# Order of VectorE's additions and of the last sums in a two-layer attention and FFN kernel

## The chip, the cores and the metric

The kernel runs on one core of one Trainium2 chip. The metric is the device time of one execution in microseconds. The core has five engines with a queue each: TensorE (PE; PEld is its weight load), VectorE (DVE), ScalarE (ACT), GpSimd (POOL) and SyncE (SP), which here issues all DMAs. Each works its queue strictly in order, and semaphores alone order one queue against another.

## The reference

2048 tokens (32 batches of 64) of width 512 pass through four stages, each with a layer norm and a residual:

```python
x = x + L0_xattn(layernorm(x), ctx, ctx, mask)          # 32 q heads, 8 kv heads, rope, softmax
x = x + L0_ffn(layernorm(x), 4-bit weights)             # silu(gate) * up, width 1376
x = x + L1_xattn(layernorm(x), ctx, mask)               # rms-normed q and k
x = x + L1_ffn(layernorm(x), ...)                       # h + gate[..., None] * aux_out
```

The last stage looks up the 8 best of 128 slots for each token (`aux_out`) and scales them with a gate that depends on a mean over all tokens. `hidden_states` there is the normed X.

## The kernel before

**Tiling.** X stays in SBUF as 16 tiles of 128 tokens x 512, named (c, t): chunk c of 512 tokens (0 to 3), tile t (0 to 3). Products of two 32-bit values are made of f16 parts, a high one and a residue ("low"), in three products. ScalarE writes the high parts, VectorE or GpSimd the residues. PB are the 8 banks of PSUM.

**The first attention** is 32 units, each a kv head g and a chunk c, software-pipelined: beside unit u the front of unit u + 1 is done. TensorE's order in one step is: `scores(u)` (L937), keys and values of u + 1 (L868, L880), the four `queries` of u + 1 (L912), the four tiles of `output(u - 1, t)` (L960), `weigh(u)` (L1002). An output tile t goes to bank 2, 3, 0, 2, and `bank()` makes TensorE wait until the last reader of a bank is through: for a tile of output this is VectorE's addition to X (`output` of VectorE, L2355). `weigh` uses banks 0, 1, 6 and 7.

Each query h is rotated: ScalarE turns it (L1547, L1548), VectorE multiplies by the cosine (L2191), GpSimd by the sine (L2962) and adds (`queries_0` of GpSimd, L2967), ScalarE makes the high part (L1554), VectorE the residue (`queries_0` of VectorE, L2200, both inputs in SBUF). `scores` of u + 1 waits for the residues 0 and 1 in its first half, 2 and 3 in its second. The softmax takes a maximum and an exponent (ScalarE, L1608) and a reciprocal.

**Work beside units** is put in by hand into numbered slots, `plan(L, u, slot, stage, ...)`; `side(L, u, slot)` in each engine's program does its part. Slot 0 is behind keys, 1 to 4 behind each query, 5 to 8 behind each output tile, 9 at the end of the unit. So `plan_ln(L, u, i, c)` puts layer norm i of chunk c into unit u, in two halves of two tiles: `ln_norm` (ScalarE, L1649, writes LNB, after GpSimd's LNR and LNK, L2946 and L2948), `ln_turn` (TensorE transposes LNB, L1031; ScalarE writes the high part of XT, L1661) and `ln_low` (VectorE, the residue of XT out of the same bank, L2158). For layer norm 1 of chunk 0, in unit 30, the second half uses banks 1 and 6. Unit 2 and unit 4 hold layer norm 0 of chunks 2 and 3. Low halves of contexts and weights are L2136.

**The end** (`last_tail`). Chunk 3 goes through the last stage tile by tile (`r_...`), the others by chunk (`t_...`). `t_norm_tile` of GpSimd (L3084) adds the normed value to X. When the gates are made (`GR`, L2638), each of the 16 tiles becomes X + GR x result. VectorE does 12, in one operation each (`t_out`, L2650): for chunks 0 and 1 the result lies in SBUF (CTB), for 2 and 3 in PSUM. Four are done by TensorE (`BY_PE`): the identity times X (L1233) and a diagonal of GR times the result (L1235) into one bank; ScalarE makes the diagonal (L1830) and copies the bank to X (L1834). The picks of chunk 3 (`r_pick`, L2666 to L2674) lie between. SP then issues one output DMA of 256 KB for each tile, in the fixed order `OUT_ORDER`, waiting for each (L832).

Of the kernel before, what the change touches and what calls it, by code (L numbers as in the profile page):

```python
# [13 lines left out]
ALU = mybir.AluOpType  # L14
# [73 lines left out]
def build(nc, din, out):  # L88
    ctx = ExitStack()
    with ctx:  # L90
# [228 lines left out]
        def eco(L, g, n):  # L319
# [34 lines left out]
        k_pow, k_mul, sql, q_pow, x_add2, tail_one = \  # L354
            [signal(n) for n in ("k_pow", "k_mul", "sql", "q_pow", "x_add2", "tail_one")]
# [76 lines left out]
        def plan_ln(L, u, i, c, early=True, last=6):  # L432

            if early:
                plan(L, u - 1, 9, "ln_stats", i, c)
            for half, (norm, turn, low) in enumerate(((0, 2, 2), (3, 5, last))):
                plan(L, u, norm, "ln_norm", i, c, half)
                plan(L, u, turn, "ln_turn", i, c, half)
                plan(L, u, low, "ln_low", i, c, half)
# [38 lines left out]
        plan_ln(0, 30, 1, 0, last=7)  # L478
# [41 lines left out]
        BY_PE = [(0, 0), (0, 2), (1, 0), (1, 2)]  # L520
        BY_DVE = [(c, t) for c in range(3) for t in range(4) if (c, t) not in BY_PE]
        SUM_BANK = {x: (7, 4)[i % 2] for i, x in enumerate(BY_PE)}
        DIAG = {x: words(128 * i, 128) for i, x in enumerate(BY_PE)}
        OUT_ORDER = [(0, 1), (0, 3), (0, 0), (1, 1), (1, 3), (0, 2), (2, 0), (1, 0), (2, 1), (2, 2), (1, 2), (2, 3)]
        OUT_ORDER += [(3, t) for t in range(4)]

# [151 lines left out]
        def sync(sp):  # L678
# [151 lines left out]
            for c, t in OUT_ORDER:  # L830
                sp.wait_ge(*((x_out, (c, t)) if (c, t) in BY_PE else (fin, (c, t))))
                sp.do.dma_start(ov[:, 4 * c + t, :], X[:, 4 * c + t, :]).then_inc(out_done.of("out", 16), 16)  # L832
# [4 lines left out]
        def tensor(pe):  # L837
# [522 lines left out]
            def last_tail():  # L1360
# [35 lines left out]
                t_out(2, 2)  # L1396
                t_sum(*BY_PE[1])
                t_out(2, 3)
                t_out(3, 2)
                t_out(3, 3)  # L1400
                t_sum(*BY_PE[2])
                t_sum(*BY_PE[3])
# [56 lines left out]
        def scalar(act):  # L1459
# [408 lines left out]
            def front(L, u, beside):  # L1868

                if L == 0:  # L1870
                    if u > 1:
                        turned_k(u)
                    exponent(0, beside)
# [200 lines left out]
        def vector(dve):  # L2074
# [615 lines left out]
            def front(L, u, beside):  # L2690
                if (L, u) != (1, 1):
                    unit_scale(L, u)
                if L == 0:
                    if u > 1:
                        turned_k(u)
                    soft_sum(0, beside)
                    if u > 1:
                        values_0(u)
                    keys_0(u)
                    side(0, beside, 0)  # L2700
                    for h in range(4):
                        turned_q(u, h)
                        if (beside, h) == (0, 3):
                            turned_p(0, 0)
                        if h == 2:
                            halved_p(0, beside, 1)
                        if h in (2, 3):
                            queries_0(u, h - 2)
                        side(0, beside, 1 + h)
                else:  # L2710
                    if beside > 0:
                        values_1(u, 0)
                        soft_sum(1, beside)
                        values_1(u, 1)
                    else:
                        soft_sum(1, 0)
                    side(1, beside, 0)
                    for h in range(4):
                        queries_1(u, h)
                        side(1, beside, 1 + h)  # L2720

            def units(L):
                for u in range(NU - 1):
# [13 lines left out]
                    for t in range(4):  # L2737
                        if u > 0:
                            output(L, u - 1, t)
                        if L == 0 and t == 0:  # L2740
                            queries_0(u + 1, 2)
# [57 lines left out]
            def last_tail():  # L2799
# [29 lines left out]
                for c, t in BY_DVE:  # L2829
                    if c < 2:  # L2830
                        t_out(c, t)
                t_out(2, 0)
                t_out(2, 1)
# [87 lines left out]
        def gpsimd(pool):  # L2921
# [167 lines left out]

            STAGE = {"join_x": join_x, "fold_x": fold_x, "fold_w": fold_w, "fold_w_halves": fold_w_halves,  # L3090
# [73 lines left out]
            def last_tail():  # L3164
# [7 lines left out]
                t_norm_tile(3, 3)  # L3172

# [99 lines left out]
```

## Time and profile before

| what | value |
|---|---|
| runs, us | 2393.34, 2393.75, 2394.59 (median 2393.75) |
| profiled execution, us | 2390.72 |
| its span, first to last instruction, us | 2388.9 |
| mean granted TensorE clock, share of full | 0.997 |
| busy PE, DVE, ACT, POOL | 98%, 73%, 54%, 54% |
| TensorE busy, 60 to 1000 us | 926.21 of 940 us |
| TensorE busy, 2345 to 2389 us | 34.17 of 44 us |
| bytes moved by DMA | 116.60 MB |

A group of instructions in the profile is a line, engine and operation; "out<-in" gives tiles. The time in brackets ahead of an instruction is its engine's idle time and what ended it; "issue" is idle time for which the trace finds no releaser. The end of a row is its start plus its duration.

### The profile page before, as it was taken

The page shows a single profiled execution, that of the slowest core. Times are in us where ns is not written, and L with a number is a line of the kernel's source. Part 1 is how long each engine was busy: PE and PEld are TensorE (multiplying, and loading weights), DVE is VectorE, ACT ScalarE, POOL GpSimd, SP SyncE. Part 2 cuts the span into 40 slices and gives each one's busy share as a digit, 9 for nine tenths or more (in the row PEclk, how much of TensorE's full clock was granted, in tenths as well). Part 3 has the DMA queues.
Part 4 walks back from the last instruction along what each step waited for, and adds up shares of the span by engine and source line. Part 5 has one row for each costly group of instructions (what it writes and reads, how often), then busy time and mean ns, then how long its engine had stood idle before and what let it go on. Part 6 is the DMA issues. An engine that isn't in the chain of part 4 may idle for free.

```text
span 2388.9 us, 46219 instructions
## 1 busy us (share of the span) xinstructions
PE 2348.3 (98%) x18028; PEld 1327.5 (56%) x18028; DVE 1740.7 (73%) x3256; ACT 1288.9 (54%) x2511; POOL 1299.4 (54%) x1042
## 2 busy tenths in 40 slices
PE   8899999999999999999999999999999999999998
PEld 4555555555555555444666655555555555555554
DVE  8887887878887898756887666666666666766666
ACT  7666565656555555424454564555555555544454
POOL 4656566666666666237763454445555555445631
PEclk9999999999999999999999999999999999999999
DMA  6121121312121111110102011222121212221101
GB/s 214 45 45 36 45 54 28 124 27 54 28 58 32 43 40 27 29 44 28 36 29 101 27 32 28 45 54 63 36 63 37 63 37 63 54 43 28 28 14 71
DMA packets 217912, 116.60 MB, mean 49 GB/s; under 512 B 169408, under 2 KB 192608, under 8 KB 216672
## 3 DMA queue, kind: packets, MB, share of 16 engines
q1 hardware_dynamic: 217696, 113.64, 18.9%
q8 instruction: 145, 2.38, 0.4%
q14 instruction: 71, 0.58, 0.1%
HBM read 65.81 MB, written 8.39 MB: 31 GB/s over the span
## 4 chain that ended last, share of the span: by engine, by line
PE 79%; DVE 9%; POOL 4%; ACT 4%; issue 3%; DMA 0%; SPq 0%; DVEq 0%; POOLq 0%; ACTq 0%
PE PB L960 24%; PE PB L912 22%; PE PB L896 6%; PE PB L1072 5%; PE PB L1129 4%; PE PB L937 3%; PE PB L1002 3%; PE PB L1083 2%; PE PB L868 2%; PE PB L880 2%; POOL AR L2962 1%; DVE AR L2340 1%; PE PB L981 1%; DVE WB L2136 1%; POOL AR L2967 1%
## 5 line engine op out<-in xcount | busy, mean ns | idle before, releaser
L960 PE MATMUL PB<-WB,AR 128*128 128x512 f16 x3072 | 682.5, 379 | 2.0 <-DVE X L2355 1.6
L912 PE MATMUL PB<-XTB,WB 128*128 128x512 f16 x3072 | 679.1, 380 | 2.6 <-DVE WB L2136 1.5
L960 PEld LDWEIGHTS PB<-WB,AR 128*128 128x128 f16 x3072 | 296.9, 98 | 356.0 <-DVE X L2355 5.0
L912 PEld LDWEIGHTS PB<-XTB,WB 128*128 128x128 f16 x3072 | 297.6, 98 | 346.6 <-issue 6.5
L2973 POOL TENSOR_TENSOR AR<-AR,SML 128x512 f32<-128x512 f32 x128 | 144.8, 1152 | 315.3 <-DVE SML L2325 315.3
L2355 DVE SCALAR_TENSOR_TENSOR X<-PB,SML,X 128x512 f32<-128x512 f32 x256 | 188.8, 746 | 165.3 <-PE PB L960 159.3
L1638 ACT ACTIVATE AR<-PB 128x512 f16<-128x512 f32 x256 | 131.6, 597 | 230.7 <-PE PB L1002 230.4
L2229 DVE TENSOR_TENSOR AR<-PB,AR 128x512 f16<-128x512 f32 x128 | 88.2, 690 | 165.1 <-ACT AR L1601 165.1
L2962 POOL TENSOR_TENSOR AR<-AR,CST 128x512 f32<-128x512 f32 x128 | 190.9, 1491 | 31.5 <-ACT AR L1548 31.5
L2967 POOL TENSOR_TENSOR AR<-AR 128x512 f32<-128x512 f32 x128 | 177.2, 1385 | 11.7 <-DVE AR L2191 1.9
L2953 POOL TENSOR_TENSOR AR<-AR,CST 128x512 f32<-128x512 f32 x32 | 49.1, 1535 | 236.2 <-ACT AR L1527 236.1
L1554 ACT ACTIVATE AR<-AR 128x512 f16<-128x512 f32 x128 | 80.5, 630 | 176.3 <-POOL AR L2967 174.8
L896 PE MATMUL PB<-WB,CTB 128*128 128x256 f16 x1536 | 173.1, 273 | 0.1
L2340 DVE TENSOR_TENSOR AR<-PB,AR 128x512 f16<-128x512 f32 x256 | 158.6, 681 | 12.8 <-ACT AR L1638 12.7
L2191 DVE TENSOR_TENSOR AR<-PB,CST 128x512 f32<-128x512 f32 x128 | 88.1, 689 | 107.7 <-ACT AR L1548 107.7
L3011 POOL TENSOR_TENSOR SML<-SML 128x16 f32<-128x16 f32 (+1 forms) x33 | 98.2, 2975 | 121.3 <-DVE SML L2237 121.3
L2200 DVE TENSOR_TENSOR AR<-AR 128x512 f16<-128x512 f32 x128 | 144.8, 1132 | 22.2 <-ACT AR L1554 22.2
L896 PEld LDWEIGHTS PB<-WB,CTB 128*128 128x128 f16 x1536 | 147.9, 98 | 17.6 <-DVE X L2355 0.4
L3003 POOL TENSOR_TENSOR AR<-AR 128x512 bf16<-128x512 f32 x128 | 147.1, 1159 | 16.1 <-ACT AR L1601 16.0
L2982 POOL TENSOR_TENSOR PSP<-AR,PSP 128x512 f16<-128x512 f32 x93 | 118.9, 1292 | 0.0
L1508 ACT ACTIVATE WB<-STG,SML 128x512 f16<-128x512 f32 (+1 forms) x164 | 92.8, 644 | 22.2 <-PE PB L960 17.4
L937 PE MATMUL PB<-AR 128*128 128x64 f16 x3072 | 102.5, 194 | 2.0 <-DVE AR L2200 2.0
(313 smaller groups left out, 4114.7 us busy)
## 6 DMA issues: line engine op xcount, KB each, us to landing
STG<-in_wo SPq DMA_DIRECT2D x14, 1024.0 KB
STG<-in_wq SPq DMA_DIRECT2D x13, 1024.0 KB
STG<-in_qw_gu SPq DMA_DIRECT2D x40, 128.0 KB
STG<-in_ctxT SPq DMA_DIRECT2D x4, 1024.0 KB
X<-in_x SPq DMA_DIRECT2D x4, 1024.0 KB, 10.5
kept<-CTB SPq DMA_DIRECT2D x4, 1024.0 KB, 7.3
CTB<-kept SPq DMA_DIRECT2D x4, 1024.0 KB, 6.5
out_x<-X SPq DMA_DIRECT2D x16, 256.0 KB, 2.4
```

Of the source, the lines that this page charges most:

```text
L896: m = pe.do.matmul(b[:, t2 * 256:(t2 + 1) * 256], CT[x][c][:, k, tok], wkv[y][:, k, :], start=n == 0, stop=n == 11)
L912: m = pe.do.matmul(b[:, :], wq[x][:, k, h * 128:(h + 1) * 128], XT[y][c][:, k, :], start=n == 0, stop=n == 11)
L937: m = pe.do.matmul(bk[:, b * SQ:(b + 1) * SQ], rows_of(QT[x], pair, b), KTT[y][:, b * SQ:(b + 1) * SQ], start=n == 0 and not by_pe, stop=n ...
L960: m = pe.do.matmul(b[:, :], AT[x][:, h, t * 128:(t + 1) * 128], wo[y][:, h, :], start=n == 0, stop=n == 11)
L1638: act.do.activation(hi, b[:, :].rearrange("p (b h q) -> p b h q", b=2, h=4), copy).then_inc(at_hi.of((L, u, j, odd)), 1)
L2200: dve.do.tensor_tensor(head_of(QT[1], h), by_batch(M1[h]), head_of(QT[0], h), ALU.subtract).then_inc(q_lo.of((0, u, h)), 1)
L2340: dve.do.tensor_tensor(lo, b[:, :].rearrange("p (b h q) -> p b h q", b=2, h=4), hi, ALU.subtract).then_inc(at_lo.of((L, u, j, odd)), 1)
L2355: dve.do.scalar_tensor_tensor(xs, PB[WB_OUT[t]][:, :], co(L, u, 0), xs, ALU.mult, ALU.add).then_inc(x_add.of((L, u, t)), 1)
L2962: pool.do.tensor_tensor(rt, rt, SINT.unsqueeze(1).to_broadcast([128, BC, SQ]), ALU.mult).then_inc(q_sin.of((u, h)), 1)
L2967: pool.do.tensor_tensor(M1[h], M1[h], RT[h], ALU.add).then_inc(q_add.of((u, h)), 1)
L2973: pool.do.tensor_tensor(v, v, RCT[:, cols].unsqueeze(2).to_broadcast([128, BC, SQ]), ALU.mult).then_inc(p_n.of((L, u, pair)), 1)
L3003: pool.do.tensor_tensor(head_of(SQL, h), by_batch(M1[h]), head_of(SQH, h), ALU.subtract).then_inc(sql.of((u, h)), 1)
```

## The change

- `OUT_ORDER` is another order of the same 16 tiles.
- Of the four tiles summed by TensorE, (0, 0) and (1, 0) go to GpSimd (`BY_GP`): a product with GR, then an addition to X, after its other work in `last_tail`. (0, 2) and (1, 2) stay with TensorE; the second of them comes behind `t_out(2, 3)`.
- VectorE sums (2, 0) and (2, 1) first, then the four tiles of chunks 0 and 1 that it had.
- In the first attention, units 2 and 4, ScalarE's first half of `ln_norm` moves from slot 0 to a new place "k", ahead of the exponent.
- In VectorE's queue the residue of query 1 moves from behind its fourth rotation to behind output 0, and that of query 2 from behind output 0 to behind output 2 (except beside unit 0).
- In unit 30 the second half of `ln_low` moves from behind output 2 to behind output 0.

```diff
@@ -351,8 +351,8 @@
             [signal(n) for n in ("ones_ok", "w_hip", "w_lop", "ln_rs", "ln_pow", "k_sin", "k_add", "p_n", "q_sin", "q_add",
                                  "uq_lo", "h_lo")]
         ph, pl, pl_dve, pt_in, kh, kl, kt_in = [signal(n) for n in ("ph", "pl", "pl_dve", "pt_in", "kh", "kl", "kt_in")]
-        k_pow, k_mul, sql, q_pow, x_add2, tail_one = \
-            [signal(n) for n in ("k_pow", "k_mul", "sql", "q_pow", "x_add2", "tail_one")]
+        k_pow, k_mul, sql, q_pow, x_add2, tail_one, gated_gp, x_gp = \
+            [signal(n) for n in ("k_pow", "k_mul", "sql", "q_pow", "x_add2", "tail_one", "gated_gp", "x_gp")]
 
 
 
@@ -433,7 +433,7 @@
 
             if early:
                 plan(L, u - 1, 9, "ln_stats", i, c)
-            for half, (norm, turn, low) in enumerate(((0, 2, 2), (3, 5, last))):
+            for half, (norm, turn, low) in enumerate((("k" if L == 0 and u < 5 else 0, 2, 2), (3, 5, last))):
                 plan(L, u, norm, "ln_norm", i, c, half)
                 plan(L, u, turn, "ln_turn", i, c, half)
                 plan(L, u, low, "ln_low", i, c, half)
@@ -475,7 +475,7 @@
                                   (27, 9, "zp", 1, 2), (28, 1, "zp", 0, 0), (28, 2, "zp", 0, 1), (28, 3, "zp", 0, 2),
                                   (28, 3, "gi", 0, 0), (28, 9, "gi", 0, 1), (29, 0, "gi", 0, 2)):
             plan(0, u, slot, name, *a)
-        plan_ln(0, 30, 1, 0, last=7)
+        plan_ln(0, 30, 1, 0, last="added")
         for k, u, slot, hi in ((0, 29, 2, 3), (1, 29, 7, 5), (2, 30, 1, 7), (3, 30, 4, 0)):
             plan(0, u, slot, "unpack", 0, k)
             if hi:
@@ -517,12 +517,12 @@
         TB_OUT = {0: (2, 3, 2, 3), 1: (0, 1, 5, 5), 2: (6, 3, 6, 3), 3: (1, 5, 0, 2)}
         RB_UP, RB_Q, RB_RA, RB_W = (1, 4, 1, 4), (3, 5, 3, 5), (0, 2, 0, 2), (7, 4, 7, 4)
 
-        BY_PE = [(0, 0), (0, 2), (1, 0), (1, 2)]
-        BY_DVE = [(c, t) for c in range(3) for t in range(4) if (c, t) not in BY_PE]
+        BY_PE, BY_GP = [(0, 2), (1, 2)], [(0, 0), (1, 0)]
+        BY_DVE = [(2, 0), (2, 1), (0, 1), (0, 3), (1, 1), (1, 3)]
         SUM_BANK = {x: (7, 4)[i % 2] for i, x in enumerate(BY_PE)}
         DIAG = {x: words(128 * i, 128) for i, x in enumerate(BY_PE)}
-        OUT_ORDER = [(0, 1), (0, 3), (0, 0), (1, 1), (1, 3), (0, 2), (2, 0), (1, 0), (2, 1), (2, 2), (1, 2), (2, 3)]
-        OUT_ORDER += [(3, t) for t in range(4)]
+        OUT_ORDER = [(2, 0), (2, 1), (0, 1), (0, 2), (0, 3), (0, 0), (1, 1), (1, 3), (3, 0), (3, 1), (1, 0), (2, 2), (1, 2), (2, 3),
+                     (3, 2), (3, 3)]
 
         def result(c, t):
             return CTB[:, c * 4096 + 1024 * t:c * 4096 + 1024 * t + 1024].bitcast(F32)
@@ -828,7 +828,7 @@
                     while rest and turn_of(rest[0]) <= (L, u):
                         bring(*rest.pop(0))
             for c, t in OUT_ORDER:
-                sp.wait_ge(*((x_out, (c, t)) if (c, t) in BY_PE else (fin, (c, t))))
+                sp.wait_ge(x_out if (c, t) in BY_PE else x_gp if (c, t) in BY_GP else fin, (c, t))
                 sp.do.dma_start(ov[:, 4 * c + t, :], X[:, 4 * c + t, :]).then_inc(out_done.of("out", 16), 16)
             sp.wait_ge(out_done, "out")
 
@@ -1394,12 +1394,10 @@
                 t_sum(*BY_PE[0])
                 r_turn_w(3)
                 t_out(2, 2)
+                t_out(2, 3)
                 t_sum(*BY_PE[1])
-                t_out(2, 3)
                 t_out(3, 2)
                 t_out(3, 3)
-                t_sum(*BY_PE[2])
-                t_sum(*BY_PE[3])
 
             keep_warm(12, 0)
             peak(("c", 0), 4)
@@ -1870,6 +1868,7 @@
                 if L == 0:
                     if u > 1:
                         turned_k(u)
+                    side(0, beside, "k")
                     exponent(0, beside)
                     if u > 1:
                         values_0(u)
@@ -2704,8 +2703,9 @@
                             turned_p(0, 0)
                         if h == 2:
                             halved_p(0, beside, 1)
-                        if h in (2, 3):
-                            queries_0(u, h - 2)
+                            queries_0(u, 0)
+                        if h == 3 and beside == 0:
+                            queries_0(u, 1)
                         side(0, beside, 1 + h)
                 else:
                     if beside > 0:
@@ -2738,6 +2738,10 @@
                         if u > 0:
                             output(L, u - 1, t)
                         if L == 0 and t == 0:
+                            side(0, u, "added")
+                            if u > 0:
+                                queries_0(u + 1, 1)
+                        if L == 0 and t == (2 if u > 0 else 0):
                             queries_0(u + 1, 2)
                         if L and t == 1 and not k_by_dma(1, u + 1):
                             keys_1(u + 1)
@@ -2827,10 +2831,7 @@
                 t_gated()
                 r_pick(3)
                 for c, t in BY_DVE:
-                    if c < 2:
-                        t_out(c, t)
-                t_out(2, 0)
-                t_out(2, 1)
+                    t_out(c, t)
                 r_sums()
                 t_out(3, 0)
                 t_out(3, 1)
@@ -3087,6 +3088,15 @@
                 t_norm_tile(c, 2 * half)
                 t_norm_tile(c, 2 * half + 1)
 
+            def t_sum(c, t):
+                n, xs = 4 * c + t, X[:, 4 * c + t, :]
+                pool.wait_ge(t_act, ("res", c, t))
+                pool.wait_ge(t_dve, "gr")
+                pool.do.tensor_scalar(result(c, t), result(c, t), GR[:, n:n + 1], None, ALU.mult).then_inc(gated_gp.of((c, t)), 1)
+                pool.wait_ge(gated_gp, (c, t))
+                pool.wait_ge(x_add2, (c, t))
+                pool.do.tensor_tensor(xs, xs, result(c, t), ALU.add).then_inc(x_gp.of((c, t)), 1)
+
             STAGE = {"join_x": join_x, "fold_x": fold_x, "fold_w": fold_w, "fold_w_halves": fold_w_halves,
                      "low": low, "ln_stats": ln_stats, "unpack_hi": unpack_hi,
                      "unpack_d": unpack_d, "t_stats": t_stats, "t_norm": t_norm}
@@ -3170,6 +3180,8 @@
                 t_stats_tile(3, 3)
                 t_norm_tile(3, 2)
                 t_norm_tile(3, 3)
+                for c, t in BY_GP:
+                    t_sum(c, t)
 
             ln_stats(0, 0)
             high(w(0, 0, 0))
```

## Rows read from the trace of the kernel before

**Rows 1.** The page of the profile, part 1: busy time and share of each engine.
```profile
PE 2348.3 (98%) x18028; PEld 1327.5 (56%) x18028; DVE 1740.7 (73%) x3256; ACT 1288.9 (54%) x2511; POOL 1299.4 (54%) x1042
```

**Rows 2.** Waits of TensorE, 60 to 1000 us: total us, times, longest.
```profile
PE PB L1031 <- ACT LNB L1649: 2.7, 2, 2.3
PE PB L1002 <- issue: 2.2, 1, 2.2
PE PB L960 <- DVE X L2355: 1.6, 3, 1.0
```

**Rows 3.** Timeline of the end: start, us, engine, line, tiles, count, [idle before].
```profile
2354.09 1.26 POOL L3084 TENSOR_TENSOR X<-X,LNB 128x512 f32<-128x512 f32 x1 [0.36 <-DVE LNB L2536]
...
2369.24 0.29 DVE L2671 SCALAR_TENSOR_TENSOR CTB<-XTB,CTB 128x128 f32<-128x128 f32 x1
...
2369.76 2.73 DVE L2650 SCALAR_TENSOR_TENSOR X<-CTB,SML,X 128x512 f32<-128x512 f32 x4
...
2380.38 0.60 ACT L1834 ACTIVATE X<-PB 128x512 f32<-128x512 f32 x1 [3.69 <-PE PB L1235]
...
2381.00 5.14 SPq L832 DMA_DIRECT2D out_x<-X  x9
...
2382.10 0.60 ACT L1834 ACTIVATE X<-PB 128x512 f32<-128x512 f32 x1 [1.12 <-PE PB L1235]
```

**Rows 4.** Timeline of unit 2 of the first attention.
```profile
110.19 0.20 POOL L2948 TENSOR_TENSOR SML<-SML 128x4 f32<-128x4 f32 x1
...
114.12 1.33 ACT L1608 ACTIVATE AR<-AR,SML 128x512 f32<-128x512 f32 x2 [4.69 <-DVE AR L2282]
...
117.38 1.50 ACT L1649 ACTIVATE LNB<-X,SML 128x512 f32<-128x512 f32 x2
...
118.32 1.33 PE L1031 MATMUL PB<-CST,LNB 128*128 128x128 f32 x8 [2.34 <-ACT LNB L1649]
```

**Rows 5.** Timeline where unit 2 hands over to unit 3.
```profile
140.04 2.75 PE L868 MATMUL PB<-CTB,WB 128*128 128x512 f16 x12 [0.56 <-DVE CTB L2136]
```

**Rows 6.** Timeline of unit 8, from its last rotations to the next scores.
```profile
310.56 1.53 DVE L2200 TENSOR_TENSOR AR<-AR 128x512 f16<-128x512 f32 x1
...
312.36 0.75 DVE L2355 SCALAR_TENSOR_TENSOR X<-PB,SML,X 128x512 f32<-128x512 f32 x1
...
313.17 2.76 PE L960 MATMUL PB<-WB,AR 128*128 128x512 f16 x12 [1.01 <-DVE X L2355]
...
315.58 0.69 DVE L2200 TENSOR_TENSOR AR<-AR 128x512 f16<-128x512 f32 x1 [0.50 <-ACT AR L1554]
...
317.28 1.57 PE L937 MATMUL PB<-AR 128*128 128x64 f16 x48
```

**Rows 7.** Timeline of unit 30.
```profile
947.79 1.18 POOL L2982 TENSOR_TENSOR PSP<-AR,PSP 128x512 f16<-128x512 f32 x1
947.87 1.64 DVE L2200 TENSOR_TENSOR AR<-AR 128x512 f16<-128x512 f32 x1
...
952.57 1.07 ACT L1661 ACTIVATE XTB<-PB 128x512 f16<-128x512 f32 x2
...
960.59 1.27 DVE L2158 TENSOR_TENSOR XTB<-PB,XTB 128x512 f16<-128x512 f32 x2
...
961.36 1.49 PE L1002 MATMUL PB<-AR 64*128 64x256 f16 x24 [2.21 <-issue]
```

**Rows 8.** Timeline of the prologue, around GpSimd's only tensor_scalar.
```profile
19.98 1.27 DVE L2158 TENSOR_TENSOR XTB<-PB,XTB 128x512 f16<-128x512 f32 x2
20.16 3.11 POOL L2926 TENSOR_SCALAR WB<-XTB,SML 128x512 f16<-128x512 f32 x2 [3.25 <-DVE SML L2104]
...
21.77 1.17 DVE L2136 SCALAR_TENSOR_TENSOR WB<-XTB,SML,WB 128x512 f16<-128x512 f32 x1 [0.52 <-POOL WB L2926]
```

**Rows 9.** The output line's view, its last line: from issue to landing.
```profile
DMA to landing us min/median/max: 2.0/2.4/3.1
```

**Rows 10.** DMA in the last 20 us, 40 slices of 0.5 us: GB/s of each.
```profile
GB/s 0 0 0 0 90 385 389 184 0 283 385 389 389 127 0 0 0 344 385 320 0 0 0 0 0 111 385 385 381 385 385 373 377 389 389 381 373 381 25 0
```

## The prediction

> **What bounds the kernel now.** I read the page first: TensorE is busy 98% of the span of 2388.9 us [rows 1]. Where it never stops, work moved on the other engines costs and gives nothing; a gain needs a stretch where TensorE stands, or the end, where it is no longer what is waited for. So I read TensorE's waits of the first attention (60 to 1000 us) next. Three belong to what is moved: for LNB by ScalarE (2.7 us, two places), for X by VectorE (1.6 us, three places), and one of 2.2 us at L1002 that the trace puts down to "issue" [rows 2]. I followed each in the timeline of its unit. At the end, I read the timeline from TensorE's last matmuls on: the SP queue issues nine of its 16 outputs from 2381.00 on, although VectorE's work on X was long under way at 2369.76 [rows 3]. The last stretch is a queue of transfers behind a tile that comes late.
>
> **First attention, ln_norm to slot "k".** In unit 2 ScalarE is idle 4.69 us until its exponent at 114.12, then it does that, values and keys, and only at 117.38 the two norms; TensorE's turn (L1031) has stood 2.34 us when it starts at 118.32 [rows 4]. The new place is ahead of the exponent. What the norm needs, LNK, is there at 110.39 (110.19 + 0.20) [rows 4], so both norms (1.50 us) end at about 111.9, inside the idle 4.69 us. They cost nothing; without that cover they would delay the exponent by 1.5 us. TensorE's 2.34 us go. ScalarE's rotations behind them come 1.5 us earlier, and VectorE's queue with them, but not 2.34. Late next: at 140.04 TensorE already waits 0.56 us for the low half of context chunk 2 (L2136) [rows 5], a VectorE step behind a long busy stretch. TensorE arrives there 2.3 earlier, VectorE some 1.4 earlier, so the wait grows by 0.9: I count 2.3 - 0.9 = **1.4** (bounds 0.4 and 2.9, the latter if that wait goes as well). Unit 4 has the same pattern with the rest of the 2.7 us, **0.4** [rows 2]. Unit 30 isn't moved (its number is over 4).
>
> **The additions to X.** After the change the residue of query 1 (L2200) stands behind output 0, that of query 2 behind output 2. In the unit around 310 us output 3 waits 1.01 us for bank 2, that is for the addition of output 0, at 312.36 to 313.11; ahead of it VectorE did the residue of query 1, 1.53 us from 310.56 [rows 6]. That is what moves behind: the addition comes about 1.4 us earlier and the wait goes. There are three such places, 1.6 us in all [rows 2]; each is at most 1.01, so I count all **1.6** (bounds 0.8 and 1.6: weigh, next in TensorE's queue, needs the addition of output 2, which comes earlier too). In the other units nothing is won, since TensorE doesn't wait there.
>
> Queued behind the added work are the residues 2 and 3 themselves, and scores of the next unit waits for them. The last one ends at 316.27; the second half of scores starts near 318.0, half-way through the 48 matmuls from 317.28 [rows 6]: 1.7 us of slack. Before the last residue VectorE even stands 0.50 us for ScalarE [rows 6]. One residue more ahead of it costs 0.69 bare; it fits.
>
> **The addition and ln_low of unit 30.** The "issue" wait is 2.21 us at 961.36. The first banks of weigh are 0 and 1, and bank 1 was last used by ln_turn(1, 0, 1), so it waits for the first of the two ln_low at 960.59, which ends at 961.23 [rows 7]. ScalarE has its half by 953.64 (952.57 + 1.07) [rows 7]. In the slot "added" the step follows output 0, about 955.5 less the residue taken out ahead of it, and ends by 956.8. Late next is the addition of output 2, which frees bank 0: from 956.8 a residue and two additions, about 0.7 each, end near 958.9, against 959.15 when TensorE is free (961.36 - 2.21). I count **2.2** (bounds 1.2 and 2.4).
>
> **GpSimd against VectorE.** The trace has a cost that the change could meet. A residue (both inputs in SBUF) takes 1.64 us from 947.87, with a GpSimd operation running from 947.79 to 948.97: it ends 0.54 us after that, where one alone takes 0.69 [rows 6, 7]. VectorE's operation with one input in PSUM doesn't feel it: two take 1.27 us under GpSimd's from 20.16 [rows 8]. So the four sums of chunks 0 and 1, which read CTB and X, can wait for GpSimd, and those of chunks 2 and 3, which read PSUM, can't.
>
> The Trainium skill, SBUF — State Buffer, "SBUF: two separate sides", has the rule: a VectorE operation with two SBUF inputs and a GpSimd operation that reads SBUF hold a shared port pair in turn, each for its whole length. By that rule the trace agrees at 947.87, but not at 21.77, where such a VectorE operation ended at 22.94, before the GpSimd operation did (23.27) [rows 8]; by the rule GpSimd's first product costs VectorE some 0.8 us and the sum below stands, by the row some 0.5 and the sum would be 0.3 more.
>
> **The end.** Removed: two of the four sums by TensorE (each two products with diagonal and identity), two diagonals and two copies by ScalarE. Added: on GpSimd, twice a product and an addition of 128x512. The addition is L3084's form, 1.26 us [rows 3]. A product f32 to f32 isn't in the trace; nearest is TENSOR_SCALAR to f16, 3.11 for two, 1.56 each [rows 8], and the addition, 1.26; I take 1.4, bounds 1.26 and 1.56. GpSimd starts when the gates are there, 0.5 us ahead of the pick's step at 2369.24, about 2368.7: tile (0, 0) is ready near 2371.5, (1, 0) near 2374.7 with VectorE in between. They stand sixth and eleventh in the new order, so they hold no transfer up.
>
> VectorE keeps its 12 sums, in another order. Now four take 2.73 us, 0.68 each [rows 3]. Without contention the seventh, (3, 0), would end at 2369.76 + 7 x 0.68 + 0.3 for the reciprocal = 2374.8 and the last at 2378.2, as TensorE no longer waits for banks 6 and 3 in the middle. With contention the pick at 2369.24 (two SBUF inputs) [rows 3] is held until the first product ends at 2370.1, some 0.8; then (0, 1) and (0, 3) wait about 1.0 each, the 1.64 less 0.69 of above. In all 2.8: (3, 0) ends near 2377.6 and the last near 2381.0.
>
> Price of the queue: 256 KB at 381 to 389 GB/s is 0.685 us [rows 10], and the fastest landing is 2.0 us after its issue [rows 9]. Before, nine from 2381.00: 2381.0 + 2.0 + 8 x 0.685 + 0.4 to the end of the span = 2388.9, as measured [rows 3]. Their cause is the fourth sum on TensorE: x_out of (1, 0) ends 2380.98 and of (1, 2) 2382.70 [rows 3], last of all tiles in X. After, with contention: eight from 2377.6, so 2377.6 + 2.0 + 7 x 0.685 + 0.4 = 2384.8, 4.1 us less. Without: all 16 back to back from 2370.5, 2370.5 + 2.0 + 15 x 0.685 + 0.4 = 2383.2, 5.7 less. The row at 947.87 is nearest to the case (both inputs f32 in SBUF), so I take **4.0**, bounds 3.0 (one more step of VectorE held for 1.0) and 5.7.
>
> The Trainium skill, GPSIMD Engine Reference, "3.1 Elementwise — side-by-side cycle accounting", speaks against the move: GpSimd takes about twice VectorE's time for an elementwise addition. Here 1.26 against 0.68; by either the two tiles are ready before their turn.
>
> **Sum.** 1.4 + 0.4 + 1.6 + 2.2 + 4.0 = 9.6 us. The profiled execution took 2390.72 us, 1.8 more than its span; less 9.6 it is 2381.1. The median of the runs is 3.0 above it, so against 2393.75 I forecast 2384.2. What a measurement can tell from no change is 0.2%, 4.8 us: below 2389.0 is faster.
>
> **The rivals.**
> A, the waits come back (9%). VectorE is the busiest helper, 73% [rows 1], and a TensorE that arrives earlier may find it no earlier, as at 140.04 [rows 5]. Then the 5.6 us of the attention shrink to 1 or less: 2393.75 - 1 - 4 = 2388.8, about no change. Against it: the wait at 961.36 has its cause moved bodily, 5 us up.
> B, contention eats the end (10%). If GpSimd's two products took the 3.1 us that the nearest row gives for a pair, each alone [rows 8], all four sums from SBUF and the pick would be caught, (3, 0) would come 3.5 us later, and 0.5 of 4.0 would stay: 2393.75 - 5.6 - 0.5 = 2387.7. Against it: by all rows GpSimd's four operations end within 6 us.
> C, slower (4%). The residues 2 and 3 stand back to back behind output 2, and each may be held by GpSimd's rotations (0.69 us alone, 1.64 held [rows 6, 7]). If the last one ends later than now by more than the 1.7 us of slack, scores waits in each of 28 units. It cancels the gain at 9.6 / 28 = 0.34 us past the slack; at 0.6 it makes 28 x 0.6 - 9.6 = 7.2 us slower, 2401. Against it: the last residue waits now for ScalarE, not for the one before it.
> D, the upper bounds together (12%): 2.9 + 0.4 + 1.6 + 2.4 + 5.7 = 13.0, so 2380.8.
> The forecast itself holds 65%.
>
> **The range.** Lower ends of the forecast's terms: 0.4 + 0.0 + 0.8 + 1.2 + 3.0 = 5.4, so 2388.4; the upper end is D's, 2380.8. That takes in the forecast, B and most of D, and leaves A and C out, with something for what I don't see. Faster: the forecast, B and D, 87%. Same: A, 9%. Slower: C, 4%.
>
> **What would show it.** L1031's waits for LNB and L960's for X gone from TensorE's list; at L868 near 138 us a wait for the context's low half of about 1.5 us; no gap at L1002 near 955. At the end, the pick L2671 near 2363 (shifted by 5.6) longer than 0.29, two or three sums from CTB of 1.3 to 1.7 us, and the SP queue issuing from start to end with no gap over 1.5 us. Wrong I am if L937 waits for L2200 in unit after unit, if the context's wait eats more than 2 us, or if the last outputs still queue behind a tile of GpSimd's.

## The result, and the profile after

The changed kernel takes 2380.80 us (median of 6 runs, 2379.67 to 2381.73), the kernel before in the same rounds 2394.28 (2393.34 to 2395.78): ratio 0.9946, 95% interval 0.9935 to 0.9956, so 10.5 to 15.6 us faster. The forecast was 2384.2, faster; the time stands on the fast edge of its range. The profiled execution took 2379.67 us with a span of 2377.8, against 2390.72 and 2388.9: 11.1 us less.

The page of the profile after, part 1; TensorE's busy time is 6.3 us less than in [rows 1], the rest of the 11.1 is time in which it stood:

```profile
PE 2342.0 (98%) x18012; PEld 1326.5 (56%) x18020; DVE 1743.2 (73%) x3256; ACT 1287.3 (54%) x2507; POOL 1289.7 (54%) x1046
```

TensorE's waits after, 60 to 1000 us. L2354, L1647 and L2157 are L2355, L1649 and L2158 of before:

```profile
PE PB L1031 <- DVE XTB L2157: 2.6, 1, 2.6
...
PE PB L1031 <- issue: 1.1, 1, 1.1
PE PB L960 <- DVE AR L2339: 1.0, 1, 1.0
PE PB L937 <- issue: 1.0, 6, 0.2
PE PB L1031 <- ACT LNB L1647: 0.6, 1, 0.6
...
PE PB L868 <- DVE X L2354: 0.2, 1, 0.2
```

The three lines of [rows 2] are gone from their places: for LNB 0.6 is left of 2.7, and at another place (937 us), X ahead of L960 is nothing, "issue" ahead of L1002 is nothing. New are 1.1 (L1031, "issue"), 1.0 (AR ahead of L960) and 0.2. The first line, at 69 us, is not the change's: the kernel before, run again (experiment 4), has 3.1 us there.

TensorE's timeline after, at the places of [rows 4 to 7]:

```profile
117.09 0.60 PE L1031 MATMUL PB<-CST,LNB 128*128 128x128 f32 x4
118.75 0.63 PE L1031 MATMUL PB<-CST,LNB 128*128 128x128 f32 x4 [1.06 <-issue]
...
139.12 2.75 PE L868 MATMUL PB<-CTB,WB 128*128 128x512 f16 x12
...
313.90 1.57 PE L937 MATMUL PB<-AR 128*128 128x64 f16 x48
315.68 2.76 PE L868 MATMUL PB<-CTB,WB 128*128 128x512 f16 x12 [0.21 <-DVE X L2354]
...
937.50 1.33 PE L1031 MATMUL PB<-CST,LNB 128*128 128x128 f32 x8 [0.56 <-ACT LNB L1647]
...
955.70 1.48 PE L1002 MATMUL PB<-AR 64*128 64x256 f16 x24
...
959.73 5.34 PE L960 MATMUL PB<-WB,AR 128*128 128x512 f16 x24 [1.04 <-DVE AR L2339]
```

A start here less that of the same instruction in [rows 4 to 7] is how far TensorE is ahead: 1.23 us at L1031, 0.92 at L868, 3.38 at L937, 5.66 at L1002. I made this difference for every matmul of both traces (count on a line against count on a line), and it changes only where an engine waits or the clock differs:

| stretch | TensorE ahead, from -> to | gain | forecast |
|---|---|---|---|
| to 110 us (clock, prologue) | 0 -> -1.27 | -1.3 | not in it |
| unit 2, to 140 | -1.27 -> 0.92 | 2.2 | 1.4 |
| unit 4, to 185 | 0.92 -> 1.74 | 0.8 | 0.4 |
| additions, to 934 | 1.74 -> 3.79 | 2.05 | 1.6 |
| unit 30, to 970 | 3.79 -> 4.68 | 0.9 | 2.2 |
| 970 to 1395 (clock) | 4.68 -> 6.18 | 1.5 | not in it |
| the end | 6.19 -> 11.1 | 4.9 | 4.0 |

The parts of the change make 10.85 us where 9.6 was forecast; the rest of the 11.1, about 0.2, is the clock's two rows, which nearly cancel.

**The end after.** I count from the end of the gates (GR, L2637 after), 2362.43 us, to the end of the span: 15.4 us, where before it was 20.3 (2368.61 to 2388.9). Timelines of VectorE, GpSimd, ScalarE and SyncE:

```profile
2363.05 0.38 DVE L2670 SCALAR_TENSOR_TENSOR CTB<-XTB,CTB 128x128 f32<-128x128 f32 x1
...
2364.98 4.52 DVE L2649 SCALAR_TENSOR_TENSOR X<-CTB,SML,X 128x512 f32<-128x512 f32 x4
...
2362.60 1.57 POOL L3095 TENSOR_SCALAR CTB<-CTB,SML 128x512 f32<-128x512 f32 x1 [13.42 <-DVE SML L2637]
2364.25 1.27 POOL L3098 TENSOR_TENSOR X<-X,CTB 128x512 f32<-128x512 f32 x1
2365.50 2.00 POOL L3095 TENSOR_SCALAR CTB<-CTB,SML 128x512 f32<-128x512 f32 x1
2367.58 1.38 POOL L3098 TENSOR_TENSOR X<-X,CTB 128x512 f32<-128x512 f32 x1
...
2369.33 0.60 ACT L1832 ACTIVATE X<-PB 128x512 f32<-128x512 f32 x1 [2.67 <-PE PB L1235]
...
2364.44 10.64 SPq L832 DMA_DIRECT2D out_x<-X  x16
...
2366.10 0.33 SPq L832 DMA_DIRECT2D out_x<-X  x1
```

And single VectorE sums from narrower stretches of the same timeline, the first and the fourth of the four:

```profile
2364.98 1.09 DVE L2649 SCALAR_TENSOR_TENSOR X<-CTB,SML,X 128x512 f32<-128x512 f32 x1
...
2367.75 1.75 DVE L2649 SCALAR_TENSOR_TENSOR X<-CTB,SML,X 128x512 f32<-128x512 f32 x1
```

GpSimd starts 0.17 after the gates. ScalarE's last copy, x_out of (1, 2), ends at 2369.93, 7.5 us after the gates; in [rows 3] it ended 14.1 after them (2382.70). SyncE's 16 issues fill 10.6 us from 2364.44 (15.6 before, from 2370.53). GB/s of the outputs after, 2358 to 2378 us, 40 slices of 0.5 us:

```profile
GB/s 0 0 0 0 0 0 0 0 16 0 0 0 0 0 160 385 393 152 381 385 381 389 385 369 377 385 90 381 385 377 385 377 377 385 393 385 365 348 0 0
```

Behind the first transfer only two slices are low, the fourth (152) and the thirteenth (90). [rows 10] has nine empty ones between its first and its last.

### The profile page after: what moved, and what is told of

The parts are those of the page before. It is cut to its first block, busy times and chain, and to the rows that moved or that the text cites. A ratio compares the mean times of both kernels' runs of the same rounds, so it can differ in the third digit from the quotient of the medians.

```text
span 2377.8 us, 46196 instructions
## 1 busy us (share of the span) xinstructions
PE 2342.0 (98%) x18012; PEld 1326.5 (56%) x18020; DVE 1743.2 (73%) x3256; ACT 1287.3 (54%) x2507; POOL 1289.7 (54%) x1046
## 4 chain that ended last, share of the span: by engine, by line
PE 79%; DVE 5%; ACT 1%; issue 1%; POOL 1%; DVEq 0%; ACTq 0%; POOLq 0%
PE PB L960 24%; PE PB L912 22%; PE PB L896 6%; PE PB L1072 5%; PE PB L1129 4%; PE PB L937 3%; PE PB L1002 3%; PE PB L880 2%; PE PB L1083 2%; PE PB L868 2%; PE PB L981 1%; PE PB L1031 1%; DVE SML L2141 1%; DVE X L2354 0%; PE PB L1182 0%
## 5 line engine op out<-in xcount | busy, mean ns | idle before, releaser
L960 PE MATMUL PB<-WB,AR 128*128 128x512 f16 x3072 | 681.4, 379 | 1.0 <-DVE AR L2339 1.0
L960 PEld LDWEIGHTS PB<-WB,AR 128*128 128x128 f16 x3072 | 297.5, 98 | 353.4 <-issue 3.1
L2354 DVE SCALAR_TENSOR_TENSOR X<-PB,SML,X 128x512 f32<-128x512 f32 x256 | 190.0, 747 | 179.1 <-PE PB L960 172.8
L2963 POOL TENSOR_TENSOR AR<-AR,CST 128x512 f32<-128x512 f32 x128 | 180.7, 1412 | 29.6 <-ACT AR L1546 29.5
L2954 POOL TENSOR_TENSOR AR<-AR,CST 128x512 f32<-128x512 f32 x32 | 47.8, 1494 | 247.2 <-ACT AR L1525 247.2
L937 PE MATMUL PB<-AR 128*128 128x64 f16 x3072 | 103.0, 194 | 3.1 <-DVE AR L2199 2.0
```

Source lines behind the costliest of these rows:

```text
L937: m = pe.do.matmul(bk[:, b * SQ:(b + 1) * SQ], rows_of(QT[x], pair, b), KTT[y][:, b * SQ:(b + 1) * SQ], start=n == 0 and not by_pe, stop=n ...
L960: m = pe.do.matmul(b[:, :], AT[x][:, h, t * 128:(t + 1) * 128], wo[y][:, h, :], start=n == 0, stop=n == 11)
L2354: dve.do.scalar_tensor_tensor(xs, PB[WB_OUT[t]][:, :], co(L, u, 0), xs, ALU.mult, ALU.add).then_inc(x_add.of((L, u, t)), 1)
L2963: pool.do.tensor_tensor(rt, rt, SINT.unsqueeze(1).to_broadcast([128, BC, SQ]), ALU.mult).then_inc(q_sin.of((u, h)), 1)
```

## The experiments

Each starts from the changed kernel unless it says otherwise. "Gates to end" is the measure above, from each kernel's own timeline. A number for the attention is TensorE's lead at one matmul, made as in the table.

**1, 2 and 4: the halves alone, and nothing.** The kernel before with the changes to the first attention (`plan_ln`, slot "k", `queries_0`, "added") alone; with those of `last_tail`, `BY_GP`, `OUT_ORDER` alone; and unedited.

> The kernel before with the three edits of the first attention alone; its end is as before. Theory (the parts add, and the attention gives what stretch by stretch the two traces show, 6.0 us): a ratio of 0.9975, and 20.3 us from the gates (GR, 128x12) to the end of the span, as before. Rival (the parts need each other, or most of the 13.5 us is not of the change): no more than 3 us faster, 0.9988 or above.

> The edits of the last stage alone; the attention is as before. Theory (the parts add): 4.9 us less, a ratio of 0.9980, and 15.4 us from the gates to the end. Rival (GpSimd in the end holds VectorE and the gain is mostly the attention's): 2 us or less, 0.9992, and over 18 us from the gates to the end.

> The kernel before, unchanged, for a second trace. Theory (the half-clock stretches of TensorE of 3.4 us each fall elsewhere in each execution and cost up to 1.7 us apiece, whatever the kernel): the same stretch-by-stretch times as in the first trace but for one to three such stretches at other places. Rival (they are tied to the work): the same places, near 53 and 1388 us of the span.

| kernel | us, median | ratio, 95% interval | gates to end |
|---|---|---|---|
| attention alone | 2386.84 | 0.9973 [0.9963, 0.9982] | 20.3 |
| end alone | 2387.76 | 0.9978 [0.9969, 0.9987] | 15.4 |
| before again | 2393.79 | 1.0004 [0.9995, 1.0013] | 20.3 |

The two halves are worth 0.27% and 0.22%, 6.5 and 5.3 us, near the 5.95 and 4.9 of the table; their sum, 11.8, lies in the interval of the whole. Neither is empty, and no loss by one another shows. The kernel before, run beside experiments 1 to 4, had a median of 2392.85 us (26 runs); beside 5 to 8 it took 2392.03 (one run), beside 9 to 12 2395.53 (nine). So a time is read only against its own rounds, and of kernels with a single run the traces are compared, not the times.

**5, 6 and 7: one part of the attention undone.**

```diff
-            for half, (norm, turn, low) in enumerate((("k" if L == 0 and u < 5 else 0, 2, 2), (3, 5, last))):
+            for half, (norm, turn, low) in enumerate(((0, 2, 2), (3, 5, last))):      # 5
...
-        plan_ln(0, 30, 1, 0, last="added")
+        plan_ln(0, 30, 1, 0, last=7)      # 6
...
-                            queries_0(u, 0)
-                        if h == 3 and beside == 0:
-                            queries_0(u, 1)
+                        if h in (2, 3):      # 7; and further down query 2 again behind output 0
+                            queries_0(u, h - 2)
```

> The changed kernel with ln_norm of units 2 and 4 back in slot 0. Theory (the norm stood behind the exponent): TensorE waits for LNB at L1031 again, 2.3 us in unit 2 and 0.4 in unit 4, and the wait for the context's low half at the start of unit 3's keys (L868 near 140 us) comes back at about 0.5; together 2.5 us more of TensorE's waits up to 200 us. Rival (VectorE, not ScalarE's norm, sets the pace of unit 2): under 1.5 us more.

> The changed kernel with the second ln_low of unit 30 back in slot 7. Theory (bank 1 waited for it): TensorE's wait ahead of L1002 near 955 us is back with 2.0 to 2.9 us, since VectorE now has one residue more ahead of slot 7, and the 1.0 us wait at L960 behind the scores of unit 31 goes. Rival (the moved additions alone cured it): under 0.5 us of wait there.

> The changed kernel with the residues of query 1 and 2 back in their old places in VectorE's queue. Theory (output 0's addition stood behind a residue): the waits of L960 for X are back, 1.0 us near 309 and 0.3 near 279 and 368, 1.6 in all, perhaps some more in unit 30, and no unit's scores change their wait. Rival (they came from something else that the change moved): under 0.5 us.

They took 2386.33, 2382.43 and 2385.10 us, one run each. TensorE's waits, 60 to 1000 us, of the fifth, the sixth and the seventh kernel:

```profile
PE PB L1031 <- ACT LNB L1647: 3.7, 3, 2.3
```

```profile
PE PB L1002 <- issue: 2.4, 1, 2.4
```

```profile
PE PB L960 <- DVE X L2354: 2.7, 4, 1.1
...
PE PB L1002 <- DVE X L2354: 1.3, 1, 1.3
```

Each brings back the wait at L1031, L1002 or L960 that it was to bring back, which shows the three mechanisms. The 0.5 at L868 that I also expected of the fifth did not come back; TensorE came there 3.1 us late, 1.7 of it by the clock, so this says little. The sizes: without "k" TensorE is 1.5 us later behind unit 2 and 1.2 more behind unit 4, 2.7 in all (4.4 in the trace, of which 1.7 is a stretch at half clock from 121 us that the trace after lacks). Without "added" it is 1.4 later at 970 us, not 2.4: the 1.0 that L960 waited for AR is gone with it (the trace shows 1.7, of which 0.35 was there at 110 us already). With the residues back it is 3.1 later, more than the 2.05 of the table. The three waits of [rows 2] are back at their places with 1.6 in all; in unit 30 there are 1.3 at L1002, for which the 0.6 at L1031 and the 1.0 for AR at L960 are gone; and a fourth wait, of 1.1, stands at 863.73. That one isn't owed to a TensorE that the other parts made early: the ninth kernel below, whose first attention is that of before, has it too, and before and before again don't. Its waits, and the place (its line numbers are one lower than those of before):

```profile
PE PB L959 <- DVE X L2354: 2.7, 4, 1.1
```

```profile
865.62 2.55 PE L959 MATMUL PB<-WB,AR 128*128 128x512 f16 x11 [1.07 <-DVE X L2354]
```

Five traces have the old order of residues. The three waits are in each of them, a fourth in three (1.1 near 865 in the seventh and the ninth, 0.3 near 489 in the second); in the nine traces with the new order L960 never waits for X. The three undone add to 2.7 + 1.4 + 3.1 = 7.2, and less the 1.3 us that TensorE loses by the fourth wait (matched starts) to 5.9, where the whole is 5.95. What brings the fourth wait on stays open.

**3, 8, 9 and 10: what the end owes to what.** Third: GpSimd's two sums on VectorE. Eighth: the old order of outputs. Ninth, from the kernel before: its own sums, the outputs in the order in which they end. Tenth: VectorE's sums out of PSUM ahead of those out of CTB.

```diff
-        BY_PE, BY_GP = [(0, 2), (1, 2)], [(0, 0), (1, 0)]
-        BY_DVE = [(2, 0), (2, 1), (0, 1), (0, 3), (1, 1), (1, 3)]
+        BY_PE, BY_GP = [(0, 2), (1, 2)], []      # 3
+        BY_DVE = [(2, 0), (2, 1), (0, 1), (0, 3), (0, 0), (1, 1), (1, 3), (1, 0)]
...
+        OUT_ORDER = [(0, 1), (0, 3), (0, 0), (1, 1), (1, 3), (0, 2), (2, 0), (1, 0), (2, 1), (2, 2), (1, 2), (2, 3)]      # 8
+        OUT_ORDER += [(3, t) for t in range(4)]
...
+        OUT_ORDER = [(0, 1), (0, 3), (1, 1), (1, 3), (0, 0), (2, 0), (2, 1), (3, 0), (3, 1), (2, 2), (0, 2), (2, 3), (3, 2), (3, 3), (1, 0), (1, 2)]      # 9
...
-                for c, t in BY_DVE:
-                    t_out(c, t)
+                t_out(2, 0)      # 10; then r_sums() and (3, 0), (3, 1), (2, 2), (2, 3), OUT_ORDER to match, and
+                t_out(2, 1)
...
+                for c, t in BY_DVE[2:]:
+                    t_out(c, t)
```

> The changed kernel, with GpSimd's two sums given to VectorE (14 sums there, (0, 0) behind (0, 3) and (1, 0) behind (1, 3)). Theory (the queue of transfers bounds the end, and GpSimd takes from VectorE by contention what it takes off it): no sum from CTB over 0.8 us, 14.6 to 15.6 us from the gates to the end, the same time as the change within 1 us. Rival (GpSimd's share is what shortens the end): at least 1.3 us longer than the change, two sums of 0.66 us each, 16.7 us from the gates to the end.

> The changed kernel with the output order of before; GpSimd's and VectorE's work as changed. Theory (the order matters where a late tile stands early; here VectorE's (0, 3) is third to fourth and (2, 0), ready first, seventh, so the queue starts 1.5 us later and (1, 0) of GpSimd is ahead of eight): 16.5 to 17.5 us from the gates to the end, against 15.4 of the change and 20.3 of before. Rival (the output order is the whole gain): 20 us.

> The kernel before with one edit: the 16 outputs are issued in the order in which its tiles become ready (the four sums of TensorE where they end), and every sum stays on its engine. Theory 1 (the end is a queue of 16 transfers fed late, and order alone feeds it): from the end of the gates to the end of the span 16.7 us in place of 20.3, so 3.6 us less than before; the rest to 15.4, 1.3 us, is what moving the two late sums off TensorE adds, since its last sum, x_out of (1, 2), still ends 11.9 us after the gates and its transfer can't end sooner than 0.685 + 2.0 + 0.4 later, with (1, 0) one ahead. Theory 2 (the sums of TensorE held the end, the order alone gives little): 19.3 to 20.3 us.

> The change, with VectorE's sums out of PSUM (2, 0), (2, 1), (3, 0), (3, 1), (2, 2), (2, 3) ahead of its four out of CTB, and the outputs in that order: GpSimd's two products and additions then lie beside sums with one input in PSUM. Theory 1 (VectorE's sums from SBUF are what GpSimd holds, 1.09, 1.17, 1.75 us in place of 0.74, and the queue's gaps of 1.07 and 1.46 us come from them): no sum of VectorE over 0.85 us, no gap of the queue over 1 us, and from the gates to the end 14.6 to 15.0 us in place of 15.4. Theory 2 (held sums are hidden by the queue): 15.3 to 15.5 us.

Kernels 8, 9 and 10 have one run each.

| kernel | sums on | order | gates to end | us |
|---|---|---|---|---|
| before | TensorE 4 | old | 20.3 | 2394.28 |
| 9 | TensorE 4 | by completion | 18.2 | 2389.68 |
| 8 | GpSimd 2, TensorE 2 | old | 17.1 | 2381.87 |
| after | GpSimd 2, TensorE 2 | new | 15.4 | 2380.80 |
| 10 | as after, PSUM first | adapted | 15.6 | 2382.18 |
| 3 | VectorE 14, TensorE 2 | new | 14.9 | 2380.88, ratio 0.9948 [0.9936, 0.9961] |

VectorE's sums out of CTB and SyncE's third issue in the third kernel:

```profile
2366.67 4.06 DVE L2649 SCALAR_TENSOR_TENSOR X<-CTB,SML,X 128x512 f32<-128x512 f32 x6
...
2367.44 0.33 SPq L832 DMA_DIRECT2D out_x<-X  x1
```

VectorE does six in 4.06 us, 0.68 each as in [rows 3], and the end is 0.5 us shorter than with GpSimd; in the time of the runs no difference can be told. So that the two sums went to GpSimd, and not to VectorE, gave nothing. What gave the 4.9 us is in the table: two sums fewer on TensorE, with VectorE's new sequence and the old order of outputs (8), are 3.2; the order of outputs alone (9) is 2.1, or 3.8 at full clock, below. So the two overlap.

The ninth kernel came out between its two expectations (16.7, and 19.3 or more), and its windows say why. Columns are the stretch and its length, TensorE's busy time, granted clock, DMA share and GB/s; then, from its timeline, ScalarE's last copy:

```profile
2376.00:2378.00 2.00, 2.00 (x4) 0.56 1.03 383
2378.00:2380.00 2.00, 2.00 (x6) 1.00 0.66 250
```

```profile
2384.84 0.60 ACT L1833 ACTIVATE X<-PB 128x512 f32<-128x512 f32 x1 [1.12 <-PE PB L1234]
```

TensorE was near its half level from 2376 to 2378 us (0.56), while it made the sums, so that the last copy starts 15.2 us after the gates (2369.66) and not 13.5 as in [rows 3] (2382.10 against 2368.61). Less these 1.7 its end is 16.5, near the 16.7 expected. One execution can't show that it would be so; the reading is that order alone gives 3.8 us at full clock and gave 2.1 here.

The tenth removed the holds as meant, and bought nothing. Its sums out of CTB, and its third and fourth issues:

```profile
2370.60 2.73 DVE L2649 SCALAR_TENSOR_TENSOR X<-CTB,SML,X 128x512 f32<-128x512 f32 x4
...
2369.01 0.83 SPq L832 DMA_DIRECT2D out_x<-X  x2
```

The four sums take 0.68 each again. But its third output is (0, 2), whose sum TensorE makes: it is issued 4.3 us after the gates (2369.01 against 2364.74), where after has 3.7 and the third kernel 3.2. From there the transfers come close behind one another, and the forecast's own formula nearly gives the end: third issue + 2.0 + 13 x 0.685 + 0.4 is 15.0, 14.5 and 15.6 for after, the third and the tenth, against 15.4, 14.9 and 15.6. In the eighth the first issue is 3.7 us after the gates, since the old order begins with a tile that VectorE now sums third: 3.7 + 2.0 + 15 x 0.685 + 0.4 = 16.4, against 17.1. So it is right to 0.1 us once and up to 0.7 short elsewhere, where the queue runs dry again behind the issue it starts from. A held sum costs only what it delays the transfers: in after the last held one leaves the slice of 90 GB/s, about 0.4 us of transfer.

**11 and 12: two that might be better.** Eleventh: "k" in unit 30 too. Twelfth: the tenth and the eleventh together.

```diff
-            for half, (norm, turn, low) in enumerate((("k" if L == 0 and u < 5 else 0, 2, 2), (3, 5, last))):
+            for half, (norm, turn, low) in enumerate((("k" if L == 0 else 0, 2, 2), (3, 5, last))):
```

> The change, with the first half of ln_norm ahead of the exponent in unit 30 too. Theory 1 (the wait of 0.56 us of L1031 for LNB at 937 us is the same thing as in units 2 and 4): that wait is gone and TensorE is 0.5 us earlier at 945 us; of it 0 to 0.5 us is left at 965 us, since TensorE waits there for VectorE's AR (1.04 us at 958.7) and arrives earlier. Theory 2 (GpSimd's LNK is late there, so that the norm holds the exponent): the exponent of unit 30 waits for LNK, and TensorE is no earlier or up to 1 us later at 945 us.

> The edits of the two kernels before this one together. Theory 1: 0.4 to 1.1 us below the change, so a ratio to the kernel before of 0.9941 to 0.9944 where the change has 0.9946; span 2376.7 to 2377.4 if the stretches of TensorE at half clock are those of the change's profiled execution. Theory 2 (both gains hidden): 0.9946, and no difference in either stretch.

The eleventh took 2380.62 us, the twelfth 2380.38 (5 runs, 2379.90 to 2380.72; ratio 0.9941, 0.9927 to 0.9955). In the eleventh L1031 no longer waits for LNB, and TensorE goes from 0.55 us behind the change's trace to 0.44 ahead. All of this 1.0 is left at 1300 us: the wait for AR stays 1.03, so VectorE had moved forward with TensorE, where my expectation had let 0 to 0.5 be left. In time neither can be told from the change.

## Why the forecast was right, and where it was off

**What held.** The gain comes from the named places in the attention and from the queue of outputs at the end; rivals A and C did not come. Of A's waits 1.06 + 1.04 + 0.56 + 0.21 us came back. For C, L937 waits for nothing but 0.16 us of "issue" in six places, and before again has that too (1.2 us in seven). D's time, 2380.8, is the measured one, but not its terms: it had 2.9 for unit 2 and 5.7 for the end, against 2.2 and 4.9, and 2.4 for unit 30, against 0.9. That the sum came out at 10.85 for 9.6 is in part luck: four terms were too small by 2.6 in all and one too large by 1.3.

**Unit 2, 1.4 -> 2.2.** The norms ran from 111.69 as forecast. The step that failed is the wait at L868, which was to grow by 0.9 and went. I took VectorE to be earlier there only by what ScalarE gives it, and its own stretch to stay as long as it was. VectorE and GpSimd before:

```profile
131.66 1.27 POOL L2967 TENSOR_TENSOR AR<-AR 128x512 f32<-128x512 f32 x1
131.69 1.78 DVE L2200 TENSOR_TENSOR AR<-AR 128x512 f16<-128x512 f32 x1 [0.23 <-ACT AR L1554]
```

The same two, VectorE's last low half and TensorE's keys in the seventh kernel, which up to here differs from before by "k" alone:

```profile
131.69 0.73 DVE L2199 TENSOR_TENSOR AR<-AR 128x512 f16<-128x512 f32 x1
...
131.96 1.60 POOL L2964 TENSOR_TENSOR AR<-AR 128x512 f32<-128x512 f32 x1
...
137.45 1.40 DVE L2135 SCALAR_TENSOR_TENSOR CTB<-STG,SML,CTB 128x512 f16<-128x512 f32 x2
...
139.07 2.75 PE L868 MATMUL PB<-CTB,WB 128*128 128x512 f16 x12
```

Before, the residue started 0.03 us behind GpSimd's addition and ended 0.54 us after it (133.47 against 132.93); in the seventh kernel it starts 0.27 ahead of it and takes 0.73, and the addition 1.60. So with the norm earlier ScalarE no longer keeps the residue waiting (0.23 us before), and it is past GpSimd's addition: 1.05 us less in VectorE's stretch, which the forecast took as fixed. The low half is done at 138.85, ahead of TensorE's 139.07, with the residues in their old places. Their new order isn't needed for it. After, it is the same with them in the new ones:

```profile
137.58 1.40 DVE L2135 SCALAR_TENSOR_TENSOR CTB<-STG,SML,CTB 128x512 f16<-128x512 f32 x2
```

It ends at 138.98, ahead of TensorE's 139.12. In exchange L1031 waits 1.06 us in its middle, which I had not foreseen. By the matched starts the unit's sum is 2.5 - 0.95 + 0.64 = 2.2. VectorE's key rotation (L2183), which reads PSUM, ends at 118.65, 0.10 before TensorE goes on; that it holds the bank is the nearest reading and wasn't tried.

**Additions, 1.6 -> 2.05.** All three waits went, which by the matched starts is 2.1; 0.4 came back at L868, and 0.3 came at 861 and 890 us. What the old order costs is itself not fixed: a fourth wait, worth 1.3, comes with it in some executions (experiment 7), and 1.6 counts only those of one trace.

**Unit 30, 2.2 -> 0.9.** The 2.2 at L1002 did go (2.2 by the matched starts too, and 0.3 just ahead of it). What I missed is what is late next, twice: L1031 at 937.50, whose norm I noted as not moved and did not follow, waits 0.56 once TensorE is 3.8 early; and behind scores L960 waits 1.04 for AR. This is the sum's worst term.

**The end, 4.0 -> 4.9.** The pick was to be held 0.8 us by GpSimd's product; it took 0.38 in place of 0.29. Two more steps were mis-sized: the product took 1.57, not 1.4, and the sums out of CTB lost 0.35, 0.4, 0 and 1.0 (against 0.74 alone), 1.8 in all against 2.0. So (3, 0) ended 8.1 us after the gates (2369.83 + 0.74), not 9.0. One reading of [rows 3] was wrong without touching the sum: the nine outputs of before stood behind x_out of (1, 0), which is the third sum on TensorE, not the fourth.

**From span to runs.** The forecast took the runs to lie 3.0 us above the profiled execution, as before. After they lie 1.1 above (2380.80 against 2379.67), which is 1.9 of the 3.4 us by which it missed. It goes with the clock, below: the fastest run after (2379.67) is the profiled one, with a mean granted clock of 0.997, and the slowest (2381.73) has 0.995. One profiled execution isn't the median execution. No term of the forecast had this. It put the time on the very edge of the range, 2380.80 against 2380.8, and that it still lies inside is luck.

## What to carry to other kernels

Where an end is a queue of transfers, its price is the first issue behind which the queue never dries, plus one transfer each: look for the tile that is late, not for the engine that is slow, and compute by that before moving work to another engine. When one wait is taken away, follow the engine that is now early through its next unit, and the helpers too: an operation that starts at another moment meets other ones. Two of my terms failed on that, one in each direction. Undo each part in the changed kernel and look at what comes back place by place: a wait that comes back can be one that the old kernel has in some executions anyway. A profile is one draw: before a difference of a few microseconds is read from two spans, the granted clock of both must be laid side by side.

## What the hardware showed beyond that

**Which GpSimd operation holds VectorE.** In the last stage, sums with both inputs in SBUF that started behind GpSimd's addition (two inputs) ended 0.55 us after it: 2366.07 after 2365.52, and 2369.50 after 2368.96, as at 947.87 in [rows 7] (0.54). The pick ran from 2363.05 to 2363.43 wholly inside GpSimd's product with one input (2362.60 to 2364.17) and lost 0.09 (0.38 for 0.29, which it takes in the third kernel, where GpSimd has nothing). The second sum out of CTB ran beside the second product and ended 0.34 ahead of it:

```profile
2365.99 1.17 DVE L2649 SCALAR_TENSOR_TENSOR X<-CTB,SML,X 128x512 f32<-128x512 f32 x1
```

It lost 0.43, and the product, 2.00 for 1.57, lost as much; in the tenth kernel, beside sums out of PSUM alone, both products take 1.57 or 1.56. So a product and a sum delay one another, but neither holds the other for its length. In the tenth kernel no sum with an input in PSUM or away from GpSimd was longer than 0.75. The Trainium skill, SBUF — State Buffer, "SBUF: two separate sides", says that whichever of the two starts first has the shared ports for its whole instruction; for GpSimd's addition the trace agrees, for its product it doesn't, and there the measurement decides.

**A clock that halves in a busy engine.** TensorE's windows of before, of after and of the fourth kernel (before again):

```profile
50.00:80.00 30.00, 25.36 (x211) 0.90 0.11 36
120.00:130.00 10.00, 10.00 (x52) 1.00 0.40 41
1375.00:1395.00 20.00, 18.51 (x195) 0.91 0.01 2
```

```profile
50.00:80.00 30.00, 24.97 (x180) 0.84 0.11 36
120.00:130.00 10.00, 10.00 (x52) 1.00 0.21 39
1375.00:1395.00 20.00, 18.51 (x203) 1.00 0.01 2
```

```profile
50.00:80.00 30.00, 24.61 (x185) 0.86 0.11 36
120.00:130.00 10.00, 10.00 (x45) 0.84 0.09 17
1375.00:1395.00 20.00, 18.51 (x195) 0.91 0.01 2
```

Mean clocks of 0.84 and 0.91 are stretches at 1.2 GHz between others at 2.4. With the same instructions (before, before again) the stretch at 120 us is there or not, although TensorE was busy all 10 us in both; at 1375 it is in before and not in after, with the same 18.51 us busy. One costs up to 1.7 us (5: from 121 us), and less where TensorE would have waited anyway (0.6 in before again, from 120 us). To 110 us, where the change shows no effect yet, TensorE is 1.27 us late in after and 1.41 in before again. They are most of what lies between the two profiled spans of one and the same kernel, 2388.9 and 2391.7, and what sets one draw off against the median. The runs say the same: of the 26 of the kernel before beside experiments 1 to 4 the fastest (2391.47) has a mean granted clock of 0.997, the three slowest (2395.44 to 2395.79) 0.994 or 0.995. The theory of experiment 4, that they fall elsewhere in each execution, failed: in the clock records of all 14 traces they come near the same places of the program, near 50 and 70 us in every one, near 1380 in 12, near 2360 in 6, near 10 in 5, near 120 in 3. What changes is whether one comes. What brings them on stays open.
